# Decay differences of a Mamba-2 layer: head by head on ScalarE in four groups a chunk, in place of two GpSimd passes

## The reference, cut to what matters

```python
xn = _layernorm(x)
# mixer
zxbcdt = xn @ w_in                       # 512 -> 1024 z, 1024 + 2*128 conv channels, 16 dt
dt = softplus(dt + dt_bias)
xBC = silu(causal_conv4(xBC))            # X (16 heads x 64), B (128), C (128)
A_cs = cumsum(dt * A)                    # per head, along the sequence
# inside a chunk, for every head: s the earlier row, l the later one
L = exp(where(s <= l, A_cs[l] - A_cs[s], -inf))
Y_diag = einsum(C, B, L, X * dt)
Y_off  = einsum(C, state, exp(A_cs))     # what earlier chunks left
y = (Y_diag + Y_off + X * D) * silu(z)
y = y * rsqrt(mean(y * y) + EPS) * norm_w
mamba = y @ w_out
# feed-forward
hidden = silu(xn @ W1.T) * (xn @ W3.T)   # 2048 wide
ffn = fwht(hidden) @ W2.T
out = x + (xn + mamba) + ffn
```

## Time and profile before

| | |
|---|---|
| time, median of 3 runs | 981.42 us (979.32 to 981.63) |
| the profiled execution | 977.44 us, its span 975.6 us, granted clock 0.99 |
| TensorE busy | 941.0 us, 96% |
| VectorE busy | 577.1 us, 59% |
| ScalarE busy | 353.4 us, 36% |
| GpSimd busy | 331.7 us, 34% |
| GpSimd L1433 and L1437, 16 times each | 58.8 and 30.3 us |

### The profile page before, as it was taken

How to read it: one execution, slowest core, us unless ns; L and a number is a source line. 1 busy time by engine, 2 the same in 40 slices (tenths; PEclk the granted TensorE clock), 3 DMA queues, 4 the chain that set the end, 5 groups by cost and what they waited for, 6 DMA issues and landing times.

```text
span 975.6 us, 13290 instructions
## 1 busy us (share of the span) xinstructions
PE 941.0 (96%) x5000; PEld 471.2 (48%) x5000; DVE 577.1 (59%) x955; ACT 353.4 (36%) x546; POOL 331.7 (34%) x370
## 2 busy tenths in 40 slices
PE   9899878998899999999999999999999999999998
PEld 4344444544444445555454445555455445555543
DVE  7876678775633766576442766576442756575521
ACT  6778755523323334222222334232221433232200
POOL 0000655562000206585210205676310204766410
PEclk9999998999999999999999999999999999999999
DMA  9798252643223435435223435445222434255122
GB/s 338 245 329 290 104 183 83 226 145 113 93 98 111 149 100 162 144 94 173 86 67 107 144 97 163 136 112 158 86 81 89 152 98 163 65 152 151 44 76 97
DMA packets 76206, 134.25 MB, mean 138 GB/s; under 512 B 7536, under 2 KB 20464, under 8 KB 74096
## 3 DMA queue, kind: packets, MB, share of 16 engines
q1 hardware_dynamic: 56640, 104.88, 33.4%
q10 hardware_dynamic: 19504, 28.53, 9.5%
HBM read 107.43 MB, written 25.95 MB: 137 GB/s over the span
## 4 chain that ended last, share of the span: by engine, by line
PE 65%; POOL 3%; DMA 2%; DVE 1%; issue 0%; DVEq 0%; ACT 0%; POOLq 0%
PE ps L594 43%; PE ps L828 14%; PE ps L790 2%; DMA arena<-cs_rows 2%; PE ps L782 2%; PE ps L776 1%; PE ps L762 1%; POOL arena L1447 1%; POOL arena L1433 1%; POOL arena L1437 0%; POOL arena L1443 0%; PE ps L613 0%; PE ps L632 0%; PE ps L745 0%; PE ps L765 0%; POOL arena L1423 0%
## 5 line engine op out<-in xcount | busy, mean ns | idle before, releaser
L594 PE MATMUL ps<-xh,arena 128*128 128x512 f16 x1592 | 490.8, 382 | 1.1 <-DVE arena L1174 0.9
L594 PE MATMUL ps<-xl,arena 128*128 128x512 f16 x796 | 303.7, 382 | 0.0
L594 PEld LDWEIGHTS ps<-xh,arena 128*128 128x128 f16 x1592 | 159.1, 100 | 190.0 <-issue 10.1
L828 PE MATMUL ps<-arena 128*128 128x512 f16 x768 | 171.1, 379 | 0.0
L1423 POOL TENSOR_TENSOR arena<-arena 128x512 f16<-128x512 f32 x64 | 82.0, 1285 | 220.7 <-ACT arena L972 220.7
L1433 POOL TENSOR_TENSOR arena<-arena 128x2048 f32<-128x2048 f32 x16 | 58.8, 3677 | 207.5 <-DMA arena<-cs_rows 207.5
L1224 DVE SCALAR_TENSOR_TENSOR arena<-ps,cw,arena 128x511 f32<-128x511 f32 (+2 forms) x120 | 89.5, 748 | 63.3 <-ACT arena L962 61.5
L594 PEld LDWEIGHTS ps<-xl,arena 128*128 128x128 f16 x796 | 78.2, 98 | 89.8 <-issue 5.0
L828 PEld LDWEIGHTS ps<-arena 128*128 128x128 f16 x768 | 74.2, 98 | 91.0 <-issue 5.5
L972 ACT ACTIVATE arena<-arena 128x512 f16<-128x512 f32 x64 | 40.3, 629 | 171.3 <-DVE arena L1245 171.3
L1240 DVE SCALAR_TENSOR_TENSOR arena<-arena,ps 128x512 f32<-128x512 f32 x64 | 43.9, 685 | 67.4 <-ACT arena L967 64.7
(11 more groups left out here) (178 smaller groups left out, 1092.3 us busy)
## 6 DMA issues: line engine op xcount, KB each, us to landing
arena<-w_parts SPq DMA_DIRECT2D x198, 256.0 KB, 2.6
w_parts<-arena SPq DMA_DIRECT2D x66, 256.0 KB, 2.4
...
```

The source lines that it names most:

```text
L594: ins = nc.tensor.matmul(out_ap, lhs(i, a), rhs(i, c), start=(i == 0 and s == 0), stop=(i == n - 1 and s == 2))
L828: ins = nc.tensor.matmul(bank(t), hw[a][:, i, t * P:(t + 1) * P], w2s[i % W2R][:, d, :], start=(i == 0 and s == 0), stop=(i == JF - 1 and ...
```

## The change

The two GpSimd passes and the marker are gone. In their place stand sixteen activations per chunk on ScalarE, one for each head: `Relu(-csbc[h] + cs_s[h])`, with the partition's own sum as a per-partition bias. That is the negated clamped difference; the exponential runs with scale -1. The sixteen are cut into four groups of four, new schedule items ES: ES 4c to 4c+3 belong to chunk c. The first group of a chunk waits for the load of `csbc`, for the sums and for TensorE's Y of the chunk before; the last one sets `esub_ok`. `ES_FIRST` and `ES_AT` place the groups; for chunk 0 of batches 1 to 3 they stand as e in `FRONT`. In batch 0 the items E of chunks 1 to 3, with their loads, move from after the tenth, eighteenth and twenty-sixth A/U tile to after the eighth, sixteenth and twenty-fourth. In batch 0 alone, SUM moves behind conv tile C4 on every engine.

```diff
--- before.py
+++ after.py
@@ -39,17 +39,18 @@
 WARM = (32, 8)
 
 
-FIRST = ("B G1S C C0 G1N C1 Z0 DT C2 DTL Z1 C3 Z2 SUM C4 Z3 WOL F0 C5 F1 SQ0 Z4 F2 C6 F3 QS0 Z5 F4 C7 F5 SQ1 Z6 F6 Z7 F7 QS1 E0 A0").split()
-FRONT = "CZCCZCZCZCZCPCZCZCPZ"
+FIRST = ("B G1S C C0 G1N C1 Z0 DT C2 DTL Z1 C3 Z2 C4 SUM Z3 WOL F0 C5 F1 SQ0 Z4 F2 C6 F3 QS0 Z5 F4 C7 F5 SQ1 Z6 F6 Z7 F7 QS1 E0 A0").split()
+FRONT = "CZCCZCZeCZeCZeCPeCZCZCPZ"
 FIRST_AT = ([("WOQ", q, q + 1) for q in range(8)] + [("WOS", 0, 10)] +
             [("WOH", q, at) for q, at in enumerate((12, 13, 13, 14, 14, 15, 16, 17))] +
             [("SQ", 2, 1), ("QS", 2, 3), ("SQ", 3, 4), ("QS", 3, 7), ("SQ", 4, 8), ("QS", 4, 12), ("SQ", 5, 11), ("QS", 5, 14),
              ("SQ", 6, 16), ("QS", 6, 20), ("SQ", 7, 20), ("QS", 7, 23)] +
             [("XL", 0, 18), ("HL", 0, 24), ("W2S", 0, 24)] +
             [("H", j, at) for j, at in enumerate((30, 31, 32, 33, 34, 35, 35, 38, 39, 40, 41, 42, 43, 44, 45, 46))])
-STEP_FIRST = {"T": (4, 12, 20, 29), "X": (6, 15, 23, 32), "S": (7, 15, 24, 33), "R": (9, 18, 26, 35), "E": (None, 10, 18, 26),
+STEP_FIRST = {"T": (4, 12, 20, 29), "X": (6, 15, 23, 32), "S": (7, 15, 24, 33), "R": (9, 18, 26, 35), "E": (None, 8, 16, 24),
               "Y": (9, 17, 26, 34), "N": (12, 20, 28, 37), "Q": (12, 20, 28, 37), "V": (14, 23, 30, 39), "W": (18, 25, 31, 41),
               "ROW": (15, 24, 31, 40)}
+ES_FIRST = (3, 4, 4, 5, 11, 12, 13, 14, 19, 20, 21, 22, 28, 29, 30, 31)
 PREP_FIRST = {"LN": 35, "XT": 42, "DT": 43, "DTL": 43, "SUM": 48}
 STEP_AT = {
     "T": (3, 7, 17, 26),
@@ -64,6 +65,7 @@
     "V": (10, 18, 26, 36),
     "W": (12, 20, 28, 38),
 }
+ES_AT = (None,) * 4 + (7, 8, 9, 10, 15, 16, 16, 17, 24, 25, 26, 27)
 PREP_AT = {"LN": 35, "XT": 40, "DT": 41, "DTL": 41, "SUM": 48}
 
 
@@ -90,6 +92,8 @@
             if f == "P":
                 seq += tiles[n:n + 2]
                 n += 2
+            elif f == "e":
+                seq.append(("ES", sum(k == "ES" for k, _ in seq)))
             else:
                 seq.append((f, (convs if f == "C" else gates).pop(0)))
             if seq[-1] == ("C", C_TILE):
@@ -101,6 +105,7 @@
         steps.append((12, 0, ("XL", 0)))
     steps += [(at, k, (kind, c)) for k, (kind, places) in enumerate(STEP_AT.items(), 1)
               for c, at in enumerate(places if b else STEP_FIRST.get(kind, places)) if at is not None]
+    steps += [(at, len(STEP_AT) + 1, ("ES", i)) for i, at in enumerate(ES_AT if b else ES_FIRST) if at is not None]
     for at, _, item in sorted(steps):
         seq += tiles[n:at]
         n = max(n, at)
@@ -241,7 +246,7 @@
         row_sq = sb("row_sq", [P, 50])
         SQ_G0, SQ_G1, SQ_WO, SQ_Q, SQ_FREE, SQ_W2 = 0, 4, 9, 18, 34, 40
         nws = sb("nws", [P, QE])
-        pool_mark, first = sb("pool_mark", [P, 1]), sb("first", [P, 1])
+        first = sb("first", [P, 1])
 
         f_in, f_half0, f_half, f_out, f_w2 = (sb(n, [P, 1]) for n in ("f_in", "f_half0", "f_half", "f_out", "f_w2"))
         f_13, f_had = sb("f_13", [P, QUADS]), sb("f_had", [P, QUADS])
@@ -415,7 +420,6 @@
         xd_ok = signal("xd_ok", NC)
         xdec_ok = signal("xdec_ok", NC - 1)
         esub_ok = signal("esub_ok", NC, 1)
-        emin_ok = signal("emin_ok", NC)
         eexp_ok = signal("eexp_ok", NC)
         m_ok = signal("m_ok", NC)
         t1_ok = signal("t1_ok", NC - 1, 1)
@@ -1042,6 +1046,17 @@
                             for r in range(2):
                                 act.dma_start(ecsb[HD * r:HD * r + HD, :].rearrange("p (q l) -> p q l", q=QE),
                                               ecs_rows[b, c].rearrange("(q r) l -> r q l", r=2)[r].partition_broadcast(HD)).then_inc(d_ecsb, 16)
+                    elif kind == "ES":
+                        c, part = divmod(i, 4)
+                        if part == 0:
+                            act.wait_ge(d_csbc, (b * NC + (c + 1)) * 16)
+                            act.wait_ge(sums_ok.sem, sums_ok.at(b, 0))
+                            act.wait_ge(pe_diag.sem, pe_diag.at(b, c - 1))
+                        for h in range(part * NH // 4, (part + 1) * NH // 4):
+                            ins = nc.scalar.activation(Eb[:, h, :], csbc[:, h, :], ACT.Relu, scale=-1.0,
+                                                       bias=cs_s[:, c * NH + h:c * NH + h + 1])
+                        if part == 3:
+                            ins.then_inc(esub_ok.sem, 1)
                     elif kind == "T":
                         if b == 0 and c == 0:
                             act.wait_ge(sq_quads, 2 * QUADS_EARLY)
@@ -1050,8 +1065,8 @@
                         act.wait_ge(pe_b.sem, pe_b.at(b, c))
                         nc.scalar.activation(Bs, bank(6)[:, 0:P], ACT.Copy).then_inc(bs_ok.sem, 1)
                     elif kind == "X":
-                        act.wait_ge(emin_ok.sem, emin_ok.at(b, c))
-                        nc.scalar.activation(Eb, Eb, ACT.Exp).then_inc(eexp_ok.sem, 1)
+                        act.wait_ge(esub_ok.sem, esub_ok.at(b, c))
+                        nc.scalar.activation(Eb, Eb, ACT.Exp, scale=-1.0).then_inc(eexp_ok.sem, 1)
                     elif kind == "S":
                         if c == 0:
                             act.wait_ge(pe_state.sem, pe_state.at(b, 0))
@@ -1421,20 +1436,6 @@
                     if kind == "U":
                         pool.wait_ge(hid_h.sem, hid_h.at(b, i))
                         nc.gpsimd.tensor_tensor(hid_lo[:, i, :], hs[i % 2], hid_hi[:, i, :], ALU.subtract).then_inc(hid_l.sem, 1)
-                    elif kind == "E":
-                        pool.wait_ge(d_csbc, (b * NC + (c + 1)) * 16)
-                        if b == 0 and c == 0:
-                            pool.wait_ge(f_done, JF // 2)
-                            pool.wait_ge(sq_w2, JF // 4)
-                            pool.wait_ge(sq_w2_dve, JF // 4)
-                        pool.wait_ge(sums_ok.sem, sums_ok.at(b, 0))
-                        pool.wait_ge(pe_diag.sem, pe_diag.at(b, c - 1))
-
-                        nc.gpsimd.tensor_tensor(Eb, csbc, cs_s[:, c * NH:(c + 1) * NH].unsqueeze(2).to_broadcast([P, NH, P]),
-                                                ALU.subtract).then_inc(esub_ok.sem, 1)
-                        pool.wait_ge(esub_ok.sem, esub_ok.at(b, c))
-                        nc.gpsimd.tensor_tensor(pool_mark[:], ones[:, 0:1], ones[:, 0:1], ALU.mult)
-                        nc.gpsimd.tensor_scalar(Eb, Eb, 0.0, -3.0e38, ALU.min, ALU.max).then_inc(emin_ok.sem, 1)
                     elif kind == "T":
                         pool.wait_ge(xt_done.sem, xt_done.at(b, MC - 1))
                         if b == 0 and c == 0:
```

## The result

The changed kernel takes 971.13 us (median of 5, 968.94 to 972.3) where the kernel before takes 979.32 us on the same chip (977.97 to 981.63): a ratio of 0.991, 95% interval 0.9888 to 0.9932. A second comparison gave 970.82 us and 0.9917 (0.9902 to 0.9932). By the profiled executions it is 971.13 us against 977.44, 6.3 us. In the four comparisons of this study the kernel before has a median of 978.8 us: the 981.42 on which the forecast rested was 2.6 us high, as its three executions fell.

The account below looks back on a forecast made before the run. TensorE's own work bounds batches 1 to 3, a chain of other engines batch 0. 1.4 (SUM) + 1.2 (W of chunk 0) + 1.4 (rest of batch 0) - 0.6 (batches 1 to 3) = 3.4 us: 981.42 becomes 978.0, range 972.5 to 983.0.

Parts of the forecast that it names:

- SUM: Batch 0 alone, moved one tile later: TensorE's idle time shrinks, gain 1.4 us, between 0 and 1.44.
- A head's pitch: ScalarE's time per 128-column Relu in a row: 0.30 us, ends 0.10 and 0.41.
- Chunk 0: Batch 0: TensorE's 4.09 us wait for `Xdec` and 1.5 us of clock go, 5.6 us given back later, net -0.8 us.
- Chunk 1: Batch 0: VectorE's low half loses 3.2 us of waiting beside GpSimd; W of chunk 0 comes 1.2 us earlier.
- The clock behind W and behind the first H: Batch 0, slow matmuls after these two waits: no term in the sum; clock loss was counted only at S.
- E3 at nothing: Batch 0, chunk 3's load: ScalarE waits for VectorE's read of `ecsb`, one tanh some 3 us late, cost nothing.
- The rest of batch 0: From N of chunk 2 to the first H: an earlier GpSimd chain and less VectorE waiting, 1.4 us, ends 0 and 2.5.
- Batches 1 to 3: Groups hidden except in chunk 2, where ScalarE waits for the load: net -0.6 us, ends +2.4 and -5.
- The base: Starting time: the profiled 977.44 us would become 974.0; the median of 981.42 becomes 978.0.
- Free room: Rival: ScalarE keeps TensorE's pace and every stall made by GpSimd's list goes, 9.4 us, so 972.0; chance 0.15.
- Only moved stalls: Rival: in batch 0 all but SUM's gain is given back at W and H, 1.2 us, so 980.2; chance 0.27.
- ScalarE as the bound: Rival: a head takes 0.40 us without overlap, making the kernel 4.6 us slower, 986.0; chance 0.18.

Follow-up runs that it names:

- e6: Changed kernel with every Relu also accumulating its row sum, an accumulator read of 0.19 us more per head, result unused: 979.47 us, ratio 1.0 to the kernel before.
- e13: Kernel before with 17 matmuls of unused result ahead of TensorE's wait at SUM of batch 0, SUM not moved: 977.86 us, ratio 1.0003.
- e11: Changed kernel with matmuls of unused result in four of TensorE's waits of batch 0: 975.17 us, ratio 0.9955 to the kernel before.

## Where the prediction was right, and the steps that failed

The mechanism of chunks 0 and 1 and of SUM came out as forecast. The step that failed most is a term put at nothing: the slow matmuls behind W of chunk 0 and behind the first H, whose waits the sum itself shortened, gave 1.7 us each. Beside it E3 was put at nothing and took 1.8 us, the flight of a load was taken as fixed, and the gain was set on a median that was 2.6 us high. In the profiles the gain of 6.3 us for 3.4 is 5.8 for 4.0 in batch 0 and 0.5 for -0.6 behind it.

- **SUM** was right: idle time at C4 2.37 us (2.3 predicted), F0 1.3 us earlier (1.4). In timed runs it is worth 2.6 to 4.7 us. Of the rest the first profile of SUM alone shows 1.7 us as the tile behind the first H, fast there by luck; the second shows none of it. The filled wait of SUM gave clock back and gained at most 1.7 us. What the rest is stays open.
- **A head's pitch** was right. Eight in a row take 2.43 us, one 0.39, so (2.43 - 0.39) / 7 = 0.29 us, for 0.30. ScalarE's timeline of batch 0, with the exponential of chunk 0 and the tanh of A4:

```profile
103.57 2.43 ACT L1056 ACTIVATE arena<-arena 128x128 f32<-128x128 f32 x8
...
110.80 1.90 ACT L1069 ACTIVATE arena<-arena 128x2048 f32<-128x2048 f32 x1
...
122.21 0.67 ACT L971 ACTIVATE arena<-ps,f 128x512 f32<-128x512 f32 x1
```

- **Chunk 0** was right in mechanism and 0.8 us too dear, by a loss that did not occur. With SUM's 1.4 us in it the exponential was forecast at 111.1 and the tanh of A4 at 123.0; they start at 110.80 and 122.21. Without SUM's gain this tanh starts when it did before: the groups cost it nothing, and QS4 is 1.4 us ahead, not 0.6.
- **Chunk 1**: the 3.2 us of the low half and QS5 came out as summed (138.29 for 140.1 less 1.4). W of chunk 0 is 3.3 us ahead for 2.6. In the ledger this is the largest step that lasts, from 1.4 us ahead at QS4 to 4.7 at QS5.
- **The clock behind W and behind the first H** is the term that was left out. The prediction itself read the earlier trace rows so, for S: four matmuls 3.46 us behind a long wait, 1.98 behind a short one. It didn't carry this to W and H, whose waits it shortened too. A wait of 3.12 us before W left 24 matmuls at 7.04 us, one of 1.81 us at 5.36; before the first H 2.72 us left the next tile at 4.44 us, 0.62 at 2.75. Twice 1.7 us, more than the 2.9 us that were missing. W's is the firmer: in every profile here that leaves this wait unfilled its matmuls were slow behind waits of 2.73 to 3.80 us and fast behind 0.79 to 2.53. At the first H the same wait went both ways: 2.73 us left the tile fast in the first run of SUM alone and 2.74 left it slow in the second profile of the kernel before, and 2.31 us did both as well.
- **E3 at nothing** was wrong. Its DMA issue waits for VectorE's read of `ecsb`, and what stands behind it in ScalarE's list waits too. ScalarE's and VectorE's timelines:

```profile
193.52 0.33 ACTq L1042 DMA_DIRECT2D arena<-cs_rows  x1
196.98 1.27 ACTq L1047 DMA_DIRECT2D arena<-ecs_rows  x2
198.37 0.72 ACT L922 ACTIVATE arena<-arena,scl 128x512 f16<-128x512 f32 x1 [4.29 <-issue]
199.00 0.67 ACT L971 ACTIVATE arena<-ps,f 128x512 f32<-128x512 f32 x1
```

```profile
195.73 1.22 DVE L1348 TENSOR_TENSOR arena<-ps,arena 128x1024 f32<-128x1024 f32 x1
...
199.70 0.69 DVE L1255 SCALAR_TENSOR_TENSOR arena<-arena,ps 128x512 f32<-128x512 f32 x1 [2.76 <-ACT arena L971]
```

  The prediction followed the tanh to its bank, which was free in time; it didn't follow VectorE, which idled 2.76 us for that tanh and had Y's and N's inputs of chunk 2 behind it. N's wait grew from 0.98 to 2.74 us, and putting the load back made it 0.98 again. How much of these 1.8 us reached the end is not shown: the times with the load back do not differ from the changed kernel's beyond their intervals.
- **The rest of batch 0** was forecast to gain 1.4 us between W of chunk 0 and the first H. It lost 0.9 behind QS6 (5.0 us ahead there, 4.1 at the first H), which E3's 1.8 more than covers. That the first H is where the forecast had it, 4.1 us ahead for about 4, is luck: W's 0.7 and its clock's 1.7 stand against these 2.3.
- **Batches 1 to 3** gained 0.5 us where a loss of 0.6 was forecast. The step that failed took a load's flight as fixed at 8.6 us. It was 9.4 in batch 2, where all went as forecast (the first group waits, W of chunk 1 then waits 1.73 us), 6.9 in batch 1, where the first group waited 1.50 us and TensorE not at all, and 5.4 in batch 3, where nothing waited. ScalarE's timeline of batch 2:

```profile
625.04 0.33 ACTq L1042 DMA_DIRECT2D arena<-cs_rows  x1
...
629.80 0.67 ACT L971 ACTIVATE arena<-ps,f 128x512 f32<-128x512 f32 x1
634.45 1.28 ACT L1056 ACTIVATE arena<-arena 128x128 f32<-128x128 f32 x4 [3.98 <-DMA arena<-cs_rows]
...
643.42 1.89 ACT L1069 ACTIVATE arena<-arena 128x2048 f32<-128x2048 f32 x1
```

- **The base**: a gain of 3.4 us, worked out on the profiled execution, was taken off a median of three executions that lay 2.6 us above the median of many. Forecast on 978.8 us, the same sum would have been 975.4, still 4.3 us above the measured time.
- **The rivals.** Free room gave 972.0, the nearest number, for a reason that is not the right one: its 5.6 us at S are given back by QS4, as the forecast said. Only moved stalls fell to QS5 and W. ScalarE as the bound fell by the pitch, and e6 shows how near it was.

What stays open: the profiles of before and after differ by 6.3 us, the medians by 8.2 and 7.65. The lost clock over the span, (1 - clock) x span, is about 11.5 us before and 7.5 after; but in e13 and e11 regained clock was not gained time, so the share of it in the 8 us isn't settled. Nor is it how the gain of the groups divides between `Xdec` and VectorE.
